# Layer with causal attention: the large matmuls in four 32-column groups of the array, the maxima turned by a transfer

## What is computed

```python
x = x + attn(layernorm(x), Wq, Wk, Wv, Wo, bo)   # 16 heads of 16, causal, scores / sqrt(256)
x = x + ffn(layernorm(x), weight, bias)          # xd @ wd.T + bias, 256 -> 256
```

## Time and profile before

| | us |
|---|---|
| median of 3 runs | 2092.31 (2090.9 to 2093.17) |
| profiled execution | 2085.36 |
| its span, first to last instruction | 2083.6 |
| TensorE busy | 1980.0 |
| VectorE busy | 1716.6 |
| ScalarE busy | 1351.9 |
| GpSimd busy | 810.7 |

### The profile page before, as it was taken

How to read it: one execution, slowest core, us unless ns; L and a number is a source line. 1 busy time by engine, 2 the same in 40 slices (tenths; PEclk the granted TensorE clock), 3 DMA queues, 4 the chain that set the end, 5 groups by cost and what they waited for, 6 DMA issues and landing times.

```text
span 2083.6 us, 35416 instructions
## 1 busy us (share of the span) xinstructions
PE 1980.0 (95%) x11749; PEld 755.4 (36%) x11749; DVE 1716.6 (82%) x4358; ACT 1351.9 (65%) x2881; POOL 810.7 (39%) x1123
## 2 busy tenths in 40 slices
PE   6799899999999999999999999999999999999984
PEld 3333333333333343434334343433333433333433
DVE  4797886869887978796897879797889899888875
ACT  5357566767766767676766666666766666677661
POOL 3323414231335554553243646453345444211232
PEclk9999999999999999999999999999999999999997
DMA  4442221414041241703323161340614121130000
GB/s 155 123 111 64 77 68 38 102 48 120 9 123 55 74 99 38 174 11 81 93 53 95 46 140 50 79 102 17 160 39 112 54 55 40 39 90 24 9 31 21
DMA packets 162963, 152.04 MB, mean 73 GB/s; under 512 B 32982, under 2 KB 150492, under 8 KB 162780
## 3 DMA queue, kind: packets, MB, share of 16 engines
q1 hardware_dynamic: 162780, 149.77, 27.0%
HBM read 91.89 MB, written 57.02 MB: 71 GB/s over the span
## 4 chain that ended last, share of the span: by engine, by line
PE 71%; DVE 19%; ACT 3%; issue 3%; POOL 2%; SPq 2%; DMA 1%; POOLq 0%; ACTq 0%; DVEq 0%
PE psum L1496 20%; PE psum L1479 19%; PE psum L1464 16%; DVE max_parts L1201 8%; PE psum L1560 8%; PE psum L1553 5%; DVE psum L1196 4%; ACT probs L1005 2%; SPq L674 1%; PE psum L1531 1%; DVE max_parts L1196 1%; ACT acc_sb L1014 1%; PE psum L1582 1%; PE psum L1523 1%; DVE stats L1259 1%
## 5 line engine op out<-in xcount | busy, mean ns | idle before, releaser
L1005 ACT ACTIVATE probs<-psum 128x512 f32<-128x512 f32 (+3 forms) x2560 | 1211.6, 536 | 518.9 <-PE psum L1479 511.8
L1201 DVE TENSOR_REDUCE max_parts<-psum 128x1 f32<-128x512 f32 x1536 | 965.2, 682 | 123.6 <-PE psum L1464 119.5
L1479 PE MATMUL psum<-q_rows,k_rows 99*128 99x512 bf16 (+3 forms) x2560 | 856.1, 351 | 3.3 <-ACT probs L1005 1.9
L1464 PE MATMUL psum<-k_rows,q_rows 96*128 96x512 bf16 (+3 forms) x2560 | 815.7, 349 | 30.2 <-DVE max_parts L1201 11.4
L1496 PE MATMUL psum<-probs,v_in 128*17 128x512 f32 (+3 forms) x5120 | 594.3, 536 | 11.9 <-ACT acc_sb L1014 11.5
L1196 DVE CUSTOM_DVE_ANT_0 psum<-psum,causal 128x128 f32<-128x128 f32 (+3 forms) x1024 | 476.5, 518 | 135.5 <-PE psum L1464 132.7
L1479 PEld LDWEIGHTS psum<-q_rows,k_rows 99*128 99x128 bf16 x2560 | 237.2, 97 | 640.5 <-ACT probs L1005 500.3
L833 POOL TENSOR_SCALAR_AFFINE_SELECT probs<-probs 128x512 f32<-128x512 f32 x256 | 165.9, 648 | 727.3 <-ACT probs L1005 727.1
L1464 PEld LDWEIGHTS psum<-k_rows,q_rows 96*128 96x128 bf16 x2560 | 244.6, 98 | 291.7 <-DVE max_parts L1201 81.8
L1496 PEld LDWEIGHTS psum<-probs,v_in 128*17 128x17 f32 x5120 | 86.1, 95 | 226.7 <-issue 162.1
L1196 DVE DVE_READ_ACCUMULATOR2_ANT max_parts<- 128x1 f32 x1024 | 144.9, 141 | 0.0
(11 more groups left out here) (161 smaller groups left out, 1268.7 us busy)
## 6 DMA issues: line engine op xcount, KB each, us to landing
q_rows<-qk_scratch SPq DMA_DIRECT2D x384, 64.0 KB, 2.7
k_rows<-qk_scratch SPq DMA_DIRECT2D x384, 64.0 KB, 2.7
qk_scratch<-shop SPq DMA_DIRECT2D x56, 384.0 KB, 3.2
sums_scratch<-acc_sb SPq DMA_DIRECT2D x48, 256.0 KB, 2.3
shop<-in_L_attn_x SPq DMA_DIRECT2D x19, 512.0 KB, 5.2
v_scratch<-shop SPq DMA_DIRECT2D x16, 544.0 KB, 4.3
v_in<-v_scratch SPq DMA_DIRECT2D x64, 136.0 KB, 2.6
out_shop<-in_L_attn_x SPq DMA_DIRECT2D x12, 512.0 KB, 8.5
```

The source lines that it names most:

```text
L1005: nc.scalar.activation(probs[s % NPROBS][:, h, a:CHUNK], bank[SCORE_BANKS[n % 3]][:, a:CHUNK], ACT.Exp, scale=SCALE).then_inc(probs_ready, 1)
L1201: nc.vector.tensor_reduce(max_parts[k % 2][:, first:first + heads, t % TILES, c], ring_bank(UNIT_USE[n])[:, 0:heads * width] .rearrange("p ...
L1464: ins = nc.tensor.matmul(dst[:, i * width:(i + 1) * width], q_rows[u][0:ROWS, qc, first + i, t % TILES * P:(t % TILES + 1) * P], k_rows[u] ...
L1479: nc.tensor.matmul(bank[SCORE_BANKS[n % 3]][:, a:CHUNK], k_rows[u][0:ROWS + LEVELS, h, kb * P:(kb + 1) * P], q_rows[u][0:ROWS + LEVELS, qc ...
```

## The change

A helper `by_columns` cuts a matmul with 128 weight columns into four, each with 32 columns and its own 32 partitions of the output. `unit`, `scores`, `project`, `linear` and `bias` use it, with the same operands as before. The transposes keep their 128 columns, and `values` is as it was. `turn_max` and `take_turned_max` are gone from TensorE and ScalarE. In their place SP issues a transposing transfer of the padded 128 x 128 bf16 tile of maxima from SBUF to SBUF, one slot after the split, and `load_max` waits for it. GpSimd waits for that transfer before it writes the same buffer again. The bf16 identity is no longer built; two tiles are cleared at the start instead.

```diff
+COLUMNS = 32
...
     p = pool(p + 1, 0.9, "split_max", k)
-    p = item(p + 1, 0.15, "turn_max", k)
-    sync(p + 1, "load_max", k)
-    assert p + 3 <= FIRSTS[k] or k < 1, (k, p, FIRSTS[k])
+    sync(p + 1, "turn_max", k)
+    sync(p + 2, "load_max", k)
+    assert p + 4 <= FIRSTS[k] or k < 1, (k, p, FIRSTS[k])
...
-        neg_max = [sbuf(f"neg_max{u}", [LEVELS, HG * TILES], BF16) for u in range(2)]
+
+        neg_wide = [sbuf(f"neg_max{u}", [P], BF16) for u in range(2)]
+        neg_max = [t[:, 0:LEVELS * HG * TILES].rearrange("p (l n) -> p l n", l=LEVELS) for t in neg_wide]
...
+            def turn_max(k):
+                sp.wait_ge(neg_ready, k + 1)
+                wait(sp, row_loaded[k % 2], 48 * (k // 2))
+                sp.dma_start_transpose(max_rows[k % 2][:, None, :], neg_wide[k % 2][:, :]).then_inc(max_turned, 16)
+
             def load_max(k):
                 g, qc = divmod(k, QC)
-                sp.wait_ge(scalar_emptied, ITEM_NO["turn_max", k])
+                sp.wait_ge(max_turned, 16 * (k + 1))
...
                 if k >= 2:
-                    pool.wait_ge(for_scalar, ITEM_NO["turn_max", k - 2])
+                    pool.wait_ge(max_turned, 16 * (k - 1))
...
-            def take_turned_max(k):
-                act.wait_ge(for_scalar, ITEM_NO["turn_max", k])
-                wait(act, row_loaded[k % 2], 48 * (k // 2))
-                nc.scalar.copy(max_rows[k % 2][0:LEVELS * HG * TILES, :],
-                               ring_bank(ITEM_USE["turn_max", k])[0:LEVELS * HG * TILES, :].bitcast(BF16)[:, 0:P]
-                               ).then_inc(scalar_emptied, 1)
...
+            def by_columns(out, weights, moving, start, stop):
+
+                for r in range(0, P, COLUMNS):
+                    ins = nc.tensor.matmul(out[r:r + COLUMNS], weights[:, r:r + COLUMNS], moving, start=start, stop=stop)
+                return ins
...
                 for i in range(heads):
-                    ins = nc.tensor.matmul(dst[:, i * width:(i + 1) * width],
-                                           q_rows[u][0:ROWS, qc, first + i, t % TILES * P:(t % TILES + 1) * P],
-                                           k_rows[u][0:ROWS, first + i, c * CHUNK:c * CHUNK + width],
-                                           start=True, stop=True)
+                    ins = by_columns(dst[:, i * width:(i + 1) * width],
+                                     q_rows[u][0:ROWS, qc, first + i, t % TILES * P:(t % TILES + 1) * P],
+                                     k_rows[u][0:ROWS, first + i, c * CHUNK:c * CHUNK + width], True, True)
...
-                nc.tensor.matmul(bank[SCORE_BANKS[n % 3]][:, a:CHUNK],
-                                 k_rows[u][0:ROWS + LEVELS, h, kb * P:(kb + 1) * P],
-                                 q_rows[u][0:ROWS + LEVELS, qc, h, a:CHUNK],
-                                 start=True, stop=True).then_inc(scores_ready, 1)
+                by_columns(bank[SCORE_BANKS[n % 3]][:, a:CHUNK], k_rows[u][0:ROWS + LEVELS, h, kb * P:(kb + 1) * P],
+                           q_rows[u][0:ROWS + LEVELS, qc, h, a:CHUNK], True, True).then_inc(scores_ready, 1)
...
-            def turn_max(k):
-                pe.wait_ge(neg_ready, k + 1)
-                use = ITEM_USE["turn_max", k]
-                emptied(pe, use)
-                nc.tensor.transpose(ring_bank(use)[0:LEVELS * HG * TILES, :].bitcast(BF16)[:, 0:P],
-                                    neg_max[k % 2][:, :, :].rearrange("p l n -> p (l n)"), identb[:, :]
-                                    ).then_inc(for_scalar, 1)
```

More of the change, by code:

```diff
@@ L377 @@
 RING = len(RING_BANKS)
-ITEM_KINDS = ("turn_max", "turn_acc", "turn_x", "project", "project_v", "turn_weights", "turn_ctx", "attend", "turn_xd",
+ITEM_KINDS = ("turn_acc", "turn_x", "project", "project_v", "turn_weights", "turn_ctx", "attend", "turn_xd",
               "feed")
-BY_SCALAR = ("turn_x", "project", "project_v", "turn_max", "turn_ctx", "turn_xd")
+BY_SCALAR = ("turn_x", "project", "project_v", "turn_ctx", "turn_xd")
 def share(things, slot, slots):
@@ L436, in layer_kernel @@
         ident = sbuf("ident", [P])
-        identb = sbuf("identb", [P], BF16)
         causal = sbuf("causal", [CHUNK])
@@ L556, in layer_kernel @@
         v_loaded = [[sem(f"v_loaded{u}_{c}") for c in range(QC)] for u in range(2)]
+        max_turned = sem("max_turned")
         row_loaded = [sem(f"row_loaded{u}") for u in range(2)]
@@ L771, in _ @@
             for p in SLOTS:
+                for k, in at("turn_max", p):
+                    turn_max(k)
                 for k, in at("load_max", p):
@@ L806, in _ @@
         def _(pool):
-            nc.gpsimd.memset(ident[:, :], 0.0)
             nc.gpsimd.memset(causal[:, :], 0.0)
             nc.gpsimd.memset(half_power[:, :], -0.5)
-            nc.gpsimd.memset(identb[:, :], 0.0).then_inc(const_step, 1)
+            for u in range(2):
+                nc.gpsimd.memset(neg_wide[u][:, :], 0.0)
+            nc.gpsimd.memset(ident[:, :], 0.0).then_inc(const_step, 1)
             pool.wait_ge(const_step, 1)
-            for m in (ident, identb):
-                nc.gpsimd.affine_select(out=m[:, :], in_=m[:, :], compare_op=ALU.not_equal, fill=1.0, base=0,
-                                        pattern=[[-1, P]], channel_multiplier=1)
+            nc.gpsimd.affine_select(out=ident[:, :], in_=ident[:, :], compare_op=ALU.not_equal, fill=1.0, base=0,
+                                    pattern=[[-1, P]], channel_multiplier=1)
             triangle = causal[:, CHUNK - P:CHUNK]
@@ L1060, in take_items @@
             def take_items(p):
-                for k, in at("turn_max", p):
-                    take_turned_max(k)
                 for n, e in at("turn_x", p):
@@ L1552, in project @@
                 for e in range(EH):
-                    ins = nc.tensor.matmul(ring_bank(use), w[:, e, (m % 2) * P:(m % 2 + 1) * P], xnT[n % 2][:, e, :],
-                                           start=e == 0, stop=e == EH - 1)
+                    ins = by_columns(ring_bank(use), w[:, e, (m % 2) * P:(m % 2 + 1) * P], xnT[n % 2][:, e, :],
+                                     e == 0, e == EH - 1)
                 ins.then_inc(for_scalar, 1)
@@ L1559, in linear @@
                     for e in range(EH):
-                        ins = nc.tensor.matmul(ring_bank(use)[:, j * E:(j + 1) * E], xT[:, e, t * P:(t + 1) * P],
-                                               w[:, e, :], start=start and e == 0,
-                                               stop=e == EH - 1 and (start or j == 1))
+                        ins = by_columns(ring_bank(use)[:, j * E:(j + 1) * E], xT[:, e, t * P:(t + 1) * P], w[:, e, :],
+                                         start and e == 0, e == EH - 1 and (start or j == 1))
                 return ins
@@ L1581, in bias @@
             def bias(use, i):
-                nc.tensor.matmul(ring_bank(use), onesb[:, :], bias_rows[i][:, None, :].broadcast_to([P, 2, E]),
-                                 start=True, stop=False)
+                by_columns(ring_bank(use), onesb[:, :], bias_rows[i][:, None, :].broadcast_to([P, 2, E]), True, False)
             def attend(n, a):
@@ L1606, in items @@
             def items(p):
-                for k, in at("turn_max", p):
-                    turn_max(k)
                 for k, in at("turn_acc", p):
```

## The result

The changed kernel takes 2030.16 us (median of 4 runs, 2024.98 to 2033.3), against 2092.74 before; the ratio is 0.970, with a 95% interval of 0.967 to 0.972. The forecast was 2054, in a range of 1990 to 2120.

The account below looks back on a forecast made before the run. TensorE's time was taken as the kernel's between slow start and tail. Its terms summed to -54 us, times 0.76 gave -41, with +3 for SP -38 on the profiled execution; hence 2054 us, range 1990 to 2120.

Parts of the forecast that it names:

- Values, -128 us: Values bursts on TensorE: neighbours now in the same mode, 0.20 us less for each of 640, -128 us.
- turn_max, -17 us: Turning of the maxima leaves TensorE: 64 times 0.26 us saved, -17 us; ScalarE's 64 small copies counted at nothing.
- Transposes, +14 us: Transposes staying in full mode: 73 bursts, each with a new switch on either side, 0.20 us each, +14 us.
- Every other matmul in four parts, +62 us: Scores, units, biases and f32 parts on TensorE: 0.01 us more for each of 6208 starts of four, +62 us.
- Rival B: Column mode on TensorE costs nothing and short loads hide: array -131 us, 1995 us at the end; chance 0.18.
- Weight loads, +15 us: TensorE's loads, one becoming four: hidden behind wide matmuls, half exposed at 512 scores and units of 128 columns, +15 us.
- Issue of instructions, hidden: TensorE's 18,560 added matmuls and as many loads: about 30 ns per instruction afterwards, taken as hidden.
- 0.76 of the array's time reaches the end: From the values line's part of the chain: 0.76 of TensorE's 54 us saving shows at the end, 41 us.
- SP's new wait, +3 us: SP waits for split maxima and the transposing transfer before row loads; first scores late at the longest chunks, +3 us.
- have several slots to spare: SP's other issues behind the new wait slip by 2 to 3 us 64 times; most were said to have slack.
- C, VectorE takes over: Rival: a busy VectorE or late row transfer eats TensorE's gain; -10 us, 2082 us; chance 0.10.
- the array's sum: All TensorE terms together, -128 - 17 + 14 + 62 + 15: -54 us.

Follow-up runs that it names:

- e4: As e2, but the maxima are turned by two bf16 matmuls with the identity in column groups instead of the transpose; 2032.1 us, ratio 0.973.
- e2: The changed kernel with turn_max back on TensorE (by a transpose) and ScalarE, so only by_columns is new; 2037.95 us, ratio 0.975.
- e3: The changed kernel with COLUMNS = 64, two groups of 64 columns in place of four of 32; 2102.7 us, ratio 1.006.
- e7: The changed kernel with each score also cut along its queries into pieces of 128, up to 16 matmuls and 16 weight loads; 2093.65 us, ratio 1.002.
- e8: The changed kernel with only scores and units in column groups; projections, linear layers and biases in the full array again; 2059.25 us, ratio 0.986.

## Why the prediction was right, and where it was not

The direction, the mechanism and the range held, but two terms of the sum were far off, in opposite directions. The profiled execution was to fall by 38 us and fell by 58. Step by step:

- *Values, -128 us.* Right, a little small. The loss on both sides is gone, and the second half is 0.43 and not 0.44, so it is 0.22 us per burst, 141 us.
- *turn_max, -17 us.* Right: between e4 and e2, which differ only in the tile of the turn, lie 14.6 us of small gaps, and its streaming was 3.4.
- *Transposes, +14 us.* Right: after the change there are 0.10 us before them and 0.09 more than before behind them.
- *Every other matmul in four parts, +62 us.* Wrong, and the largest error. The 0.01 us was a trait of the values beside neighbours of another tile size. In e3 the halves of the values are 0.014 apart beyond their columns again, in the changed kernel 0.005. Rival B had this right.
- *Weight loads, +15 us.* Wrong: nothing. A matmul of 128 bf16 columns is followed by the next one with a median of 4 to 5 ns beyond its columns, before and after. The Trainium skill's "TensorEngine Tiling (Array Packing)", section Restrictions and Gotchas, says that column tiling excludes the fast weight load. The trace doesn't show the loss (a load of 32 columns is recorded with 97 ns, one of 128 had 98), and the loads were hidden.
- *Issue of instructions, hidden.* Right for this kernel. e7 got by with 7 ns or less in a short run and with 19 ns, and some pauses, over a whole kernel. The Trainium skill's "TensorE: Matmul & The Clock Gate", section Back-to-back issue gap, gives about 62 ns per MATMUL where firmware decodes. That isn't the case here: e7 averages 38 ns per matmul with its load.
- *0.76 of the array's time reaches the end.* Wrong by as much as the +62, the other way: 62 of 139 us, 0.45. It was the share of a chain measured while TensorE was slow. e8 shows that 0.88 or more is possible for a small difference (29 to 33 of 33); for the large one the stalls come in.
- *SP's new wait, +3 us.* Near: TensorE waits 3.9 us for the row. That slower-moving transfers behind it "have several slots to spare" was wrong for the sums and the stores.
- *C, VectorE takes over.* In part: about 18 us.

So two large errors cancelled for the most part: 77 us that were not paid, against a share of 0.45 and not 0.76. For the array's sum rival B was right (-131 us, measured -139; the forecast had -54), and with the forecast's share that would have been 1995 us. That 2030 lies nearer to 2054 is luck. How much of the missing share belongs to SP's queue and how much to VectorE is open beyond the 18 us; the stalls behind SP's transfers are seen, but no run took them away.

## What to carry to other kernels

Where narrow and full matmuls alternate on TensorE, look at the distance of starts on both sides of the narrow ones. If it is 0.10 us too long, put all of them into the narrow ones' tile size; here, with 33 ns for each instruction, that cost nothing. A tile size between the two (e3) didn't help.

A share of the chain of waits is no price for a large change. When one engine gets 7% faster, ask which queue that runs in order was nearly late, SP's too: here a load that VectorE waited 5.5 us for cost TensorE 5.65 us, and the half clock after them.

## What the runs showed of the hardware

- The switch between column tile sizes: in the kernel before the values start 0.096 us later than the columns of the matmul ahead need, and what follows them 0.098 us later than their last part needs (medians at full clock). With 64-column neighbours (e3) it is 0.100 and 0.096 us.
- In tiles of 64 columns (e3) a quarter of the starts of scores and units come 0.02 us or more later than the columns need. In the changed kernel it is 4%, in the kernel before 3% (at full clock, waits left out).
- A transposing transfer of 128 x 128 bf16 within SBUF holds SP for 1.1 us, a plain one for 0.43 to 0.59. SP then waited 68.5 us in 53 of 64 cases, 1.3 us each:

```profile
L690 SPq DMA_TRANSPOSE max_rows<-neg_max x64: 1108/1129/2233, 69.3 to 1918.3; - x64
```
```profile
SPq L697 <- DMA max_rows<-neg_max: 68.5, 53, 3.7
```
